# Making the turned copy of U by DMA instead of by a product, with apply two units ahead, in a frequency-domain orthogonal convolution

## The reference

```python
x = x + conv(groupnorm(x), weight, bias)      # x: 32 x 128 x 32 x 32, fp32

def conv(x, weight, bias):                    # n = 34, nf = 18: 612 frequencies, 580 of them distinct
    xfft = rfft2(pad(x))                      # (frequency, cin, batch)
    v    = rfft2(weight)                      # (frequency, 128, 127), complex
    w    = vH @ v + eps * I
    W    = I - 2 * (v @ solve(w, vH))         # one complex linear solve of size 127 per frequency
    z    = irfft2(W @ xfft)
    return z[..., 1:-1, 1:-1] + bias
```

## Time and profile before

| | |
|---|---|
| median of 3 runs | 2848.31 us (2847.0 to 2858.18) |
| profiled execution, first to last instruction | 2851.4 us |
| TensorE matmul busy | 2466.2 us (86%) |
| VectorE busy | 1900.5 us (67%) |
| ScalarE busy | 1390.0 us (49%) |
| the 16 sweeps, first apply to last VectorE update | 709.3 us |

### The profile page before, as it was taken

How to read it: one execution, slowest core, us unless ns; L and a number is a source line. 1 busy time by engine, 2 the same in 40 slices (tenths; PEclk the granted TensorE clock), 3 DMA queues, 4 the chain that set the end, 5 groups by cost and what they waited for, 6 DMA issues and landing times. The chain is left out here.

```text
span 2851.4 us, 89547 instructions
## 1 busy us (share of the span) xinstructions
PE 2466.2 (86%) x37953; PEld 2018.1 (71%) x37953; DVE 1900.5 (67%) x4779; ACT 1390.0 (49%) x3469; POOL 503.3 (18%) x872
## 2 busy tenths in 40 slices
PE   4975977999999899998987978787888888997999
PEld 4954744666566687777866767675776776987998
DVE  6852446888979768585768888897886885002444
ACT  1422422344353466665764646464565563772332
POOL 0002412121310011111111101010322221440000
PEclk7977988999999999999998989898899999997999
DMA  5274476331411283663835334361312323555874
GB/s 193 90 127 85 77 144 157 113 122 68 154 45 44 37 165 77 120 121 70 170 62 102 74 77 96 56 122 31 112 61 61 113 69 115 165 164 125 213 215 138
DMA packets 562604, 310.03 MB, mean 109 GB/s; under 512 B 484616, under 2 KB 495496, under 8 KB 561368
## 3 DMA queue, kind: packets, MB, share of 16 engines
q1 hardware_dynamic: 520896, 183.58, 30.7%
q0 software_dynamic: 41312, 120.73, 13.1%
HBM read 162.85 MB, written 141.30 MB: 107 GB/s over the span
## 5 line engine op out<-in xcount | busy, mean ns | idle before, releaser
L1499 DVE SCALAR_TENSOR_TENSOR arena<-arena,psum 128x512 f32<-128x512 f32 (+2 forms) x608 | 399.0, 720 | 322.5 <-PE psum L1063 322.4
L1063 PE MATMUL psum<-arena 32*128 32x128 f32 (+1 forms) x9280 | 300.4, 274 | 13.7 <-ACT arena L1250 9.7
L1040 PEld LDWEIGHTS psum<-arena 32*32 32x32 f32 x9280 | 162.0, 137 | 202.6 <-issue 201.1
L1063 PEld LDWEIGHTS psum<-arena 32*128 32x128 f32 x9280 | 279.0, 186 | 35.1 <-ACT arena L1250 20.3
L1002 PE MATMUL psum<-arena 128*32 128x256 f32 (+1 forms) x3696 | 262.7, 379 | 35.0 <-DMA arena<-plain 27.9
L1211 ACT COPY arena<-arena 32x128 f32<-32x128 f32 (+2 forms) x608 | 244.6, 402 | 92.4 <-DVE arena L1510 71.9
L1446 DVE TENSOR_TENSOR arena<-arena 128x320 f32<-128x320 f32 (+6 forms) x600 | 260.5, 485 | 8.2
L1040 PE MATMUL psum<-arena 32*32 32x64 f32 x9280 | 184.4, 231 | 89.2 <-DVEq L1491 78.7
L941 POOL COPY arena<-arena 128x512 f32<-128x512 f32 (+2 forms) x160 | 86.1, 584 | 830.1 <-ACT arena L1211 830.1
L1110 PE MATMUL psum<-arena 128*128 128x160 f32 x1160 | 198.8, 314 | 28.2 <-ACT arena L1290 28.1
L998 PE MATMUL psum<-arena 128*32 128x256 f32 (+1 forms) x2576 | 214.5, 401 | 9.9 <-DVE arena L1499 6.9
(11 more groups left out here) (126 smaller groups left out, 5020.6 us busy)
## 6 DMA issues: line engine op xcount, KB each, us to landing
blocks<-arena POOLq DMA_DIRECT2D x145, 256.0 KB, 2.3
arena<-blocks SPq DMA_DIRECT2D x290, 128.0 KB, 2.8
kept<-arena POOLq DMA_DIRECT2D x145, 256.0 KB, 3.1
arena<-kept SPq DMA_DIRECT2D x145, 256.0 KB, 3.0
xhat<-arena SPq DMA_DIRECT2D x32, 580.0 KB, 14.9
arena<-xhat SPq DMA_DIRECT2D x580, 32.0 KB, 2.6
yhat<-arena POOLq DMA_DIRECT2D x290, 64.0 KB, 2.5
arena<-x SPq DMA_DIRECT2D x8, 2048.0 KB, 9.8
```

What stands on the lines that cost most here:

```text
L1040: ins = pe.matmul(psum[0][h, L * t:L * t + L], ce[h, sj % NCE, :, slot + t], M[h, home(q) + t, c, :], start=True, stop=True)
L1063: ins = pe.matmul(upd_bank(u, c)[:, L * t:L * (t + m)].rearrange("p (a q m) -> p a q m", a=m, q=LB), rows.rearrange("p q r m -> p (q r m)" ...
L1499: ins = dve.scalar_tensor_tensor(old, old, K["mask"][:, piv:piv + 1], upd_bank(u, c)[:, 0:L * n].rearrange("p (t n) -> p t n", n=L), ALU.m ...
```

## The change

The turned copy is no longer a product. ScalarE writes U twice from PSUM: once multiplied by a sign per partition (+1 on even partitions, -1 on odd ones) into `signed`, once plainly into the unit. Two DMAs of SyncE then copy the signed U into the unit, each from every other partition to its neighbour. For this `place` now writes the factors so that real and imaginary rows alternate by partition. The unit's layout is new: the quad index t is innermost, so that a DMA row is 4 x n x B bytes long (512 for 8 quads), and what `update` reads as weights and as moving columns lies n elements apart (32 bytes for 8 quads).

There are three unit buffers (one in `emb`, two in `work`) and two for `signed`. Two PSUM banks now take U, and `apply` runs two units ahead of `update`. SyncE issues the DMAs in its program order, so the loads of the next stage come behind a sweep's last turn, and the loads of "form" and "pre" wait for the end of the sweep before. ScalarE waits for stores from `work` before it writes a unit there.

```diff
+    c["sign"] = np.where(i % 2 == 0, 1.0, -1.0)[:, None]
...
+                    def turn_u(u):                                  # SyncE
+                        n = B * sweep_units[u][1]
+                        sp.wait_ge(S["u_signed"], u + 1)
+                        if used_before[u] >= 0:
+                            sp.wait_ge(S["upd_done"], used_before[u] + 1)
+                        for r in range(2):
+                            sp.dma_start(every_other(UNIT_AT[slot_of[u]] + n, r, [2 * n, LB], [1, n]),
+                                         every_other(SIGNED_AT[u % 2], 1 - r, [n, LB], [1, n])).then_inc(S[f"ju_in{slot_of[u]}"], 16)
...
+                            if before("sweep", at):                 # SyncE, ahead of the loads of form and pre
+                                sp.wait_ge(S["upd_done"], before("sweep", at))
...
-                        if u:
-                            pe.wait_ge(S["u_copied"], u)
+                        if u >= 2:
+                            pe.wait_ge(S["u_copied"], u - 1)
...
-                                ins = pe.matmul(psum[0][h, L * t:L * t + L], ce[h, sj % NCE, :, slot + t],
+                                ins = pe.matmul(psum[u % 2][h, L * t:L * t + L], ce[h, sj % NCE, :, slot + t],
...
-                        pe.matmul(psum[1][:, 0:L * n], K["nturn"],
-                                  u_emb[:, u % 2, 0:n].rearrange("p t q r m -> p (t q) r m")[:, :, 0, :],
-                                  start=True, stop=True).then_inc(S["j_turned"], 1)
...
-                        pe.wait_ge(S["ju_copied"], u + 1)
+                        pe.wait_ge(S["u_copied"], u + 1)
+                        pe.wait_ge(S[f"ju_in{slot_of[u]}"], landed_by[u])
...
-                                rows = u_emb[quadrant(cls(p, c)), u % 2, t]
+                                rows = unit(u)[quadrant(cls(p, c)), :, :, :, t]
...
-                                                rows.rearrange("p q r m -> p (q r m)"), spread(real_half(rows), 1, m),
+                                                rows.rearrange("p q r m -> p (q r m)"), spread(rows[:, :, 0, :], 1, m),
...
-                            turn_u(lo)
+                            apply(lo + 1)
                             for u in range(lo, hi):
-                                if u + 1 < hi:
-                                    apply(u + 1)
+                                if u + 2 < hi:
+                                    apply(u + 2)
                                 update(u)
-                                if u + 1 < hi:
-                                    turn_u(u + 1)
...
+                    def copy_signed(u):                             # ScalarE, ahead of copy_u(u)
+                        act.wait_ge(S["u_done"], u + 1)
+                        if u >= 2:
+                            act.wait_ge(S[f"ju_in{slot_of[u - 2]}"], landed_by[u - 2])
+                        act.activation(signed(u).rearrange("p q m t -> p (q m) t"), by_column(u), ACT.Copy,
+                                       scale=K["sign"]).then_inc(S["u_signed"], 1)
+
+                    def copy_u(u):
+                        if used_before[u] >= 0:
+                            act.wait_ge(S["upd_done"], used_before[u] + 1)
+                        act.copy(unit(u)[:, :, 0, :, :], by_column(u).rearrange("p (q m) t -> p q m t", q=LB)).then_inc(S["u_copied"], 1)
+
+                    def by_column(u):
+                        n = sweep_units[u][1]
+                        return psum[u % 2][:, 0:L * n].rearrange("p (t a) -> p a t", t=n)
...
-                            link(dve.transpose(to[:, B * piece:B * piece + B, :], pieces[:, at]))
+                            link(dve.transpose(to.rearrange("p (m r) s -> p r m s", r=2)[:, piece], pieces[:, at]))
```

More of the change, by code:

```diff
@@ L665, in build, with carve_at @@
         scaled_row = a(NT, 3 * B)
+        EMB_AT = a.at
         emb = a(2, 2, QUAD, LB, 2, B)
-        u_emb = emb.rearrange("p a b f q r m -> p a (b f) q r m")
         at = a.at
+        part_in = a(4, QUAD, 2 * L)
+        WORK_AT = a.at
         work = a(2, QUAD, 4 * L)
-        part_in = a(4, QUAD, 2 * L)
+        UW = 8 * L
+        def carve_at(at, *shape):
+            return Carve(at)(*shape)
+        UNIT_AT = [EMB_AT, WORK_AT, WORK_AT + 2 * UW]
+        SIGNED_AT = [EMB_AT + 2 * UW, EMB_AT + 3 * UW]
         carve = lambda v, at, *shape: v.rearrange("p a f n -> p (a f n)")[:, at:at + int(np.prod(shape))].rearrange(
@@ L777, in build @@
                 jobs.append((kind, g, k, at, len(where)))
+        slot_of, landed_by, used_before = {}, {}, {}
+        for at_, (kind, g, k, lo, hi) in enumerate(jobs):
+            if kind == "sweep":
+                mids = [j[4] for j in jobs[:at_] if j[0] == "mid"]
+                turns = [0, 2, 1] if mids and mids[-1] % 2 else [0, 1, 2]
+                for u in range(lo, hi):
+                    slot = turns[(u - lo) % 3]
+                    earlier = [v for v in slot_of if slot_of[v] == slot]
+                    slot_of[u], landed_by[u] = slot, 32 * (len(earlier) + 1)
+                    used_before[u] = max(earlier, default=-1)
         def last_part(kind, g, k):
@@ L822, in upd_bank, with unit, signed, every_other @@
             return psum[2 + (QUAD * u + c) % 6]
-        def real_half(e):
-            return e[:, :, 0, :]
+        ROW = list(arena[:, 0:1].ap[0])[0]
+        def unit(u):
+            n = sweep_units[u][1]
+            return carve_at(UNIT_AT[slot_of[u]], LB, 2, B, n)
+        def signed(u):
+            n = sweep_units[u][1]
+            return carve_at(SIGNED_AT[u % 2], LB, B, n)
+        def every_other(at, r, *dims):
+            return bass.AP(arena, r * ROW + at, [[2 * ROW, P // 2], *dims])
         names = ["ccoef_in", "pre_done", "pre_copied", "formed", "form_copied", "gathered", "taken", "chain", "factored", "reset",
-                 "u_done", "u_copied", "upd_done", "added", "upd_copied",
-                 "j_turned", "ju_copied", "b_copied", "p_copied", "turned", "j_copied", "t_done", "t_copied", "s_done", "s_copied",
+                 "u_done", "u_signed", "u_copied", "upd_done", "added", "upd_copied",
+                 "b_copied", "p_copied", "turned", "j_copied", "t_done", "t_copied", "s_done", "s_copied",
                  "q_turned", "q_copied", "q_beside", "jq_copied", "z_done", "z_copied", "y_done", "y_copied"]
@@ L833, in build @@
         names += [f"bx_in{n}" for n in range(3)] + [f"pre_stored{n}" for n in range(NST)] + [f"tail_in{n}" for n in range(NTAIL)]
-        names += [f"part_in{n}" for n in range(4)] + [f"tile_in{n}" for n in range(6)]
+        names += [f"ju_in{n}" for n in range(3)] + [f"part_in{n}" for n in range(4)] + [f"tile_in{n}" for n in range(6)]
         with ExitStack() as es:
@@ L905, in _ @@
                                     store_half(sp, 1)
+                        elif kind == "sweep":
+                            for u in range(lo, hi):
+                                turn_u(u)
                         elif kind == "mid":
@@ L1039, in apply, with update @@
                                 h = quadrant(cls(p, c))
[L1040 removed]
+                                ins = pe.matmul(psum[u % 2][h, L * t:L * t + L], ce[h, sj % NCE, :, slot + t],
                                                 M[h, home(q) + t, c, :], start=True, stop=True)
                         ins.then_inc(S["u_done"], 1)
[L1044 removed]
+                    def update(u):
                         q, n, p, sj = sweep_units[u]
                         pe.wait_ge(S["u_copied"], u + 1)
[L1047 to L1055 removed]
+                        pe.wait_ge(S[f"ju_in{slot_of[u]}"], landed_by[u])
                         if u:
@@ L1237, in pivot_pieces, with work_stored @@
                         return out
-                    def copy_u(u):
-                        q, n, p, sj = sweep_units[u]
+                    def copy_signed(u):
                         act.wait_ge(S["u_done"], u + 1)
                         if u >= 2:
[L1243 to L1251, removed]
+                            act.wait_ge(S[f"ju_in{slot_of[u - 2]}"], landed_by[u - 2])
[6 more added lines that the diff above has]
+                    def by_column(u):
+                        n = sweep_units[u][1]
+                        return psum[u % 2][:, 0:L * n].rearrange("p (t a) -> p a t", t=n)
+                    def work_stored(at, u):
+                        done = mid_quads[0:before("mid", at)]
+                        for n in range(2):
+                            if slot_of[u] == n + 1 and done[n:]:
+                                act.wait_ge(S[f"part_stored{n}"], 16 * len([q for q in done if q % 2 == n]))
+                            if slot_of[u] == 2 and before("final", at):
+                                act.wait_ge(S[f"y_stored{n}"], 32 * len(final_quads[n:before("final", at):2]))
                     def copy_blocks(m):
@@ L1343, in _ @@
                         elif kind == "sweep":
```

(13 more changed lines are left out.)

2 lines of the change are left out of this document (1 added, 1 removed).

## The result

The changed kernel takes 3094.05 us (median of 4, 3087.6 to 3101.22) beside 2847.65 us (2844.0 to 2858.18) for the kernel before: a ratio of 1.084, 95% interval 1.0805 to 1.0876 (the two medians alone give 1.087). Slower was forecast, but 2930 us and at most 2970. The mechanism named was there; its size was too small, and a wait that the prediction did not have, the larger of the two misses, came on top.

The account below looks back on a forecast made before the run. The prediction took TensorE as the bound, 4.06 us a unit with the removed product on its path. 2851 - 160 (product and smaller terms) + 243 (stepped read) = 2934, 3 less for the runs' median: 2930 us, range 2690 to 2970.

Parts of the forecast that it names:

- The stepped read: In update, weights and moving columns 32 bytes apart: 56.5 ns a record instead of 30.3, +243 us (bounds 186 and 278).
- the step costs nothing at half clock: Rule from apply's weight loads, 128 bytes apart: at half clock 168 ns against 177, not longer.
- The turns: The product removed from TensorE's path in the sweeps: 138 us of turns and 14 of waits, together -152 us.
- The sweep starts: First apply to first update takes 5.4 or 6.2 us, DMAs uncovered; five warm starts pay 1.4 each, +7 us.
- ScalarE: Per unit: signed copy 0.7 us for one of 0.6, 3.0 in all, hidden; PSUM step of 64 elements costs nothing.
- The DMAs: Each turn's second DMA lands some 3.5 us after the signed copy: hidden in steady state, uncovered at a sweep's start.
- SyncE's order: Loads of later stages issued behind a sweep's last turn, and those of the inverse transform: balance about 0.
- That the step costs nothing: Rival: update's stepped reads are free, a unit is 3.0 us of TensorE, 2700 us in all; chance 0.27.
- half: Rival: update's stepped reads cost 12 to 20 ns a record, 2800 to 2875 us in all; chance 0.10.
- That both reads take turns: Rival: update's stepped weights and moving columns can't be read at once, some 110 ns a record, 3430 us; chance 0.07.
- That the DMAs come late: Rival: DMAs never land within 5 us, each unit waits, 300 us without a step cost, 3000 us; chance 0.04.

Follow-up runs that it names:

- step1: The changed kernel with quads outermost, so update reads contiguously and DMAs move 64-byte pieces: 2895.91 us, 1.0137 times the kernel before.
- step4: The changed kernel with four quads interleaved, a step of 16 bytes in update's reads and DMA pieces of 256 bytes: 3106.52 us (one run).
- step2: The changed kernel with two quads interleaved, a step of 8 bytes in update's reads and DMA pieces of 128 bytes: 2878.97 us, 1.0052 times the kernel before.
- layout_only: The kernel before with only the quad index innermost in the unit's layout, its product and order kept, no DMA turn: 3128.84 us (one run).
- seven: The changed kernel with apply one unit ahead in one PSUM bank and updates rotating through seven banks instead of six: 3022.37 us, 1.0585 times the kernel before.
- moving_step: From `seven`, two unit buffers instead of three, update's weights contiguous (64-byte DMA rows), moving columns still stepped: 3107.38 us (one run).

## Why the prediction was right in kind and wrong in time

Two steps failed: the cost of the stepped read was set 50 us too low, and the wait for VectorE, 96 us, was put at nothing without a reason. Together they are 146 of the 164 us between 2930 and 3094.

**The stepped read: mis-sized.** +243 was forecast (bounds 186 and 278), +293 measured, and +291 with the layout alone. The step that failed is the one that took the extra time of a column from a load of 32 columns: 20 ns, corrected to 30, that is 0.63 to 0.94 ns a column. On 128 columns it is (332 - 183) / 128 = 1.16 ns. A likely reason, not tested, is that part of a short load lies beside work that the step does not lengthen, so that 32 columns showed only the rest. The slope between two sizes gives it: stepped (332 - 128) / 96 = 2.1 ns a column, contiguous 0.8. I took twice the contiguous rate; it is 2.7 times. A second row would have warned. An update of the kernel before that lies mostly at half clock (granted 0.61) shows what contiguous loads take there:

```profile
L1063 PEld LDWEIGHTS psum<-arena x64: 182/328/328, 1688.6 to 1691.4; 32*128 32x128 f32 x64
```

328 ns, the length that a stepped load has at full clock. And the stepped update does not get longer at half clock, as the 168 against 177 ns of the earlier trace rows had said; two updates of one sweep of the changed kernel, columns as above:

```profile
719.62:723.60 3.98, 3.98 (x64) 1.00 0.23 66
731.04:735.02 3.98, 3.98 (x64) 0.54 0.19 49
```

For a load the step does what half clock would do. For the update it does more, since a contiguous one at half clock, here in `step1`, takes 3.33 us where the stepped one takes 3.98. The prediction's rule that the step costs nothing at half clock holds for the load alone:

```profile
1204.50:1207.83 3.33, 3.33 (x64) 0.50 0.81 89
```

A record of 64 thus costs 63 ns inside an update (4.03 us), not 56.5.

By "TensorE: Matmul & The Clock Gate", "LDWEIGHTS (loading the stationary operand)", of the Trainium skill a load is priced by its columns alone; with 128 columns each, the loads of `step4` (327 ns) and of the changed kernel (332) against those of `step1` (183) contradict it; those of `step2` (194) hardly do.

**The turns: right in size.** The product is gone, and `layout_only` with its product has a period of 565.05 - 558.91 = 6.14 where `seven` without has 5.10: 1.04, beside the 1.06 forecast.

**The wait for VectorE: a term that was missing.** In the changed kernel half of the 1.06 came back as a wait. The step that failed is the one that took the removed product off the period whole, and looked for new waits on the DMAs alone. It named no work that had lain under the product, and there was some: turn and apply, 2.1 us, covered the 1.5 to 1.7 that VectorE needs to free the shared PSUM banks. Apply alone leaves 0.55 open, or 0.77 behind the shorter apply of a 6-quad unit, 85 times, 49 us. At the end of a sweep the order two ahead has no apply left, and the last two updates wait 1.3 us and more, 32 times, 47 us. All that is needed stood in the earlier trace rows and in the new order: VectorE begins 0.14 behind an update and takes 0.68 for each of the first two instructions. The sum with both corrections is -160 + 293 + 96 = +229, beside +233 in the sweeps. The lower clock needs hardly a term, since the stepped update takes 3.98 us at either level; only apply grows, by 192.6 - 184.4 = 8 us of busy time. `step1`, whose updates are contiguous, does pay for it.

**The sweep starts: right as a sum, with some luck.** +7 forecast, measured 50.70 + 43.87 = 94.6 against 88.5, +6. But 5.4 to 6.2 us were forecast everywhere, and the sixteen run from 4.8 to 7.8.

**ScalarE: right.** 0.7 forecast for the signed copy, 0.69 in the timeline; the plain copy takes 0.58. Its reading of PSUM with a step of 64 elements costs nothing: `step1` reads without it and has 0.69 and 0.61.

**The DMAs: right.** Landing after 2.4 us (3 forecast), hidden in mid-sweep. At the sweep starts, where nothing was to cover them, TensorE waits for them 21.5 us, which is part of the starts above.

**SyncE's order: right.** Near 0 forecast, -0.5 measured between the sweeps.

**The rivals.** That the step costs nothing, or half, is refuted by every kernel that has one of 16 bytes or more. Had it cost nothing, 2700 us would still have been out of reach: `step1` is that case, and has 2896. Its sweeps take 731.6 us, where the rival has 709 - 160 + 10 = 559. The wait for VectorE (85 us), the gaps in the middle of a product (30), starts of 117.3 us where 95.5 were forecast (22, with 64-byte pieces that land after 4.5 us), 43 more at the update and 8 more at apply make 188 beside a difference of 173, with some counted twice where a gap lies in a start. Most of the 43 is the clock: 36 updates of `step1` run at least in part at the lower level, 8 in the kernel before, and one that does so whole takes 3.3 us instead of 1.9. That both reads take turns would have needed 110 ns a record; the changed kernel has 63. That the DMAs come late is refuted by the changed kernel too, which in mid-sweep never waits for them.

**Left open.** What opens the 30 us of gaps in the middle of the products of `step1` was not found. Nor is it known why three updates of `step2` take 2.5 to 2.6 us at full clock. The banks of `seven` with the reads of `step1` or `step2` were not tried together. No version beat the kernel before; `step2`, which pays 11 ns a load for rows of twice the length, comes nearest at 1.0052, and keeps 107 us of waiting for VectorE.

## What to carry to other kernels

When a product is taken off the critical engine, list what had to happen while it ran, and compare that with what is left between the same two instructions; here the next wait stood ready 0.5 us behind. Do so at the ends of the loop too: an order that runs two steps ahead has nothing to put between its last two. When a profile calls a gap "issue", look at what the program waits for there before you give it a cause. When a layout is chosen for a transfer, ask how many elements of each line its reader will still use: for fp32 in a matrix product a step of two elements cost 6% more for each load and one of four 80%. Size such a cost from two lengths of the same operation, not from one short one.

## What the runs showed that I had not expected

The cost of a step in a TensorE read is a threshold: 183, 194, 327, 332 ns at steps of 4, 8, 16 and 32 bytes. The loads at 327 and more are as long as contiguous ones at half clock (328), but the update around them is longer (3.98 us against 3.33). Stepping the weights or the moving columns alone costs nearly as much as stepping both (62 and 58 ns a record against 63), though with stepped moving columns the loads stay at 204 ns. The SBUF-to-SBUF copies of 128 KB landed after 2.4 us in pieces of 512 bytes, 3.1 in pieces of 128 and 4.0 (`moving_step`) to 4.5 (`step1`) in pieces of 64. A wait for a DMA stood in the profile as "issue" in 15 of 16 sweep starts of `step1`.
